# Cross-attention with LoRA on one core: where four of the eight Wkv tiles get their raw weight in the opening

## The reference

```python
def _lora_linear(x, W, A, B):
    return x @ W + 2.0 * (x @ A @ B)
q = _lora_linear(hidden, Wq, Aq, Bq)        # 8 x 256 x 1024
k = _lora_linear(traces, Wk, Ak, Bk)        # 8 x 256 x 256
v = _lora_linear(traces, Wv, Av, Bv)        # 8 x 256 x 256
scores = q @ k.T / sqrt(32)                 # per head
context = softmax(scores) @ v
out = hidden + _lora_linear(context, Wo, Ao, Bo)
```

## Time and profile before

| | |
|---|---|
| median of 3 runs | 675.79 us (675.72 to 678.38) |
| the profiled execution, its own time | 678.06 us |
| its span in the trace | 676.3 us |
| mean granted TensorE clock | 0.947 |
| PE, DVE, ACT, POOL busy | 98%, 76%, 69%, 56% of the span |

### The profile page before, as it was taken

How to read it: one execution, slowest core, us unless ns; L and a number is a source line. 1 busy time by engine, 2 the same in 40 slices (tenths; PEclk the granted TensorE clock), 3 DMA queues, 4 the chain that set the end, 5 groups by cost and what they waited for, 6 DMA issues and landing times.

```text
span 676.3 us, 13385 instructions
## 1 busy us (share of the span) xinstructions
PE 662.5 (98%) x4220; PEld 528.2 (78%) x4220; DVE 512.7 (76%) x1161; ACT 467.6 (69%) x1462; POOL 375.9 (56%) x325
## 2 busy tenths in 40 slices
PE   9999999999999999999999999999899999999998
PEld 6798777877877887887887788787676788888886
DVE  4768887787788778778777877878887898855542
ACT  5558888888888888888888888887678443222220
POOL 3548785843762584386358438535867005776632
PEclk9999999999999999999999999999899999999999
DMA  8956655675665567556656646667676335655331
GB/s 268 355 171 211 207 182 164 196 212 167 174 197 183 158 195 227 162 179 195 198 149 201 210 157 183 197 187 211 186 225 205 107 120 172 202 187 186 126 121 66
DMA packets 103829, 125.07 MB, mean 185 GB/s; under 512 B 9280, under 2 KB 85312, under 8 KB 103760
## 3 DMA queue, kind: packets, MB, share of 16 engines
q1 hardware_dynamic: 103760, 124.23, 59.6%
HBM read 86.18 MB, written 38.01 MB: 184 GB/s over the span
## 4 chain that ended last, share of the span: by engine, by line
PE 82%; DVE 8%; ACT 4%; DMA 3%; issue 2%; SPq 1%; DVEq 0%
PE banks L1484 20%; PE banks L1677 17%; PE banks L1482 10%; PE banks L1502 9%; PE banks L1532 8%; PE banks L1519 8%; PE banks L1543 6%; DVE neg_max L1142 2%; ACT banks L930 2%; PE banks L1463 2%; DVE turned_sb L1163 2%; DMA raw<-xt 1%; PE banks L1450 1%; DVE max_parts L1151 1%; DMA raw<-ct 1%
## 5 line engine op out<-in xcount | busy, mean ns | idle before, releaser
L930 ACT ACTIVATE banks<-banks,neg_max 128x256 f32<-128x256 f32 x512 | 229.9, 452 | 29.8 <-DVE neg_max L1142 24.6
L812 POOL TENSOR_TENSOR q_stack<-turned_sb,head_mask 8x512 fp32r<-8x512 f32 x128 | 136.0, 1062 | 172.8 <-DVE turned_sb L1163 167.1
L1142 DVE TENSOR_REDUCE neg_max<-banks 128x2 f32<-128x512 f32 x256 | 175.0, 686 | 41.9 <-PE banks L1502 38.9
L941 ACT ACTIVATE probs_t<-banks 128x512 f32<-128x512 f32 x256 | 155.0, 605 | 48.4 <-PE banks L1519 48.0
L1484 PE MATMUL banks<-x_both,w_hi 128*128 128x512 f32 x448 | 162.9, 396 | 0.1
L1482 PE MATMUL banks<-x_both,w_lo 128*128 128x256 f32 x448 | 118.6, 280 | 0.0
L1502 PE MATMUL banks<-k_stack,q_stack 96*128 96x256 f32 x512 | 109.8, 296 | 0.7 <-DMA q_stack<-q_parts 0.7
L1502 PEld LDWEIGHTS banks<-k_stack,q_stack 96*128 96x128 f32 x512 | 81.3, 190 | 35.4 <-issue 25.8
L930 ACT ACTIVATION_READ_ACCUMULATOR banks<-banks,neg_max 128x1 f32 x512 | 106.7, 208 | 0.0
L1519 PE MATMUL banks<-q_stack,k_stack 104*128 104x512 f32 x256 | 102.4, 400 | 0.0
L1482 PEld LDWEIGHTS banks<-x_both,w_lo 128*128 128x128 f32 x448 | 84.5, 189 | 9.2
(11 more groups left out here) (156 smaller groups left out, 1154.7 us busy)
## 6 DMA issues: line engine op xcount, KB each, us to landing
q_stack<-q_parts SPq DMA_DIRECT2D x192, 128.0 KB, 3.0
q_parts<-q_stage SPq DMA_DIRECT2D x64, 256.0 KB, 3.5
raw<-ct SPq DMA_DIRECT2D x32, 256.0 KB, 3.5
raw<-xt SPq DMA_DIRECT2D x32, 256.0 KB, 3.8
scales<-r_rows SPq DMA_DIRECT2D x64, 128.0 KB
context<-ctx_stage SPq DMA_DIRECT2D x64, 128.0 KB, 3.7
stage<-xn SPq DMA_DIRECT2D x16, 512.0 KB, 5.4
w_hi<-context SPq DMA_DIRECT2D x14, 512.0 KB, 7.0
```

The lines of the kernel that those rows point to most:

```text
L812: nc.gpsimd.tensor_tensor(q_stack[rows, u % RING, heads], turned_sb[rows, u % 2].unsqueeze(1).broadcast_to([M_ROWS, 2, S]), head_mask[rows ...
L930: last = nc.scalar.activation(score_bank(s)[:, S * h:S * (h + 1)], score_bank(s)[:, S * h:S * (h + 1)], ACT.Exp, bias=neg_max[:, u % 2, i: ...
L941: nc.scalar.activation(probs_t[:, u % 2, t, 2 * hp:2 * hp + 2, :].rearrange("p a b -> p (a b)"), st_bank[j % 2], ACT.Exp, scale=-1.0).then ...
L1142: nc.vector.tensor_reduce(out=neg_max[:, u % 2, 2 * c:2 * c + 2], in_=score_bank(s).rearrange("p (h t) -> p h t", h=2), axis=AXIS, op=ALU. ...
```

## The change

Wkv's tiles 1, 3, 5 and 7 go the second way (PE multiplies only A by B, DVE adds the raw weight, POOL makes the low part); tiles 0, 2, 4 and 6 stay. DVE's order in the opening becomes: `w_total(1)`, `w_low(0)`, `w_total(3)`, `w_low(2)`, `w_total(5)`, `w_low(4)`, context quarters 0 and 1, `w_total(7)`, `w_low(6)`, context quarters 2 and 3. POOL makes the four low parts between its first and its second stack. ACT's order is the same.

```diff
+KV_ADDS = (0, 2, 4, 6)
...
         def pe_adds(f):
-            return f < FOLD_Q or f in (FOLD_Q + 1, FOLD_Q + 3, FOLD_Q + 5, FOLD_Q + 7, FOLD_Q + 8, FOLD_Q + 12)
+            return f in KV_ADDS or f in (FOLD_Q + 1, FOLD_Q + 3, FOLD_Q + 5, FOLD_Q + 7, FOLD_Q + 8, FOLD_Q + 12)
...
             stack_lows(0)
+            for f in range(FOLD_Q):
+                if not pe_adds(f):
+                    w_low(f)
+            pool.wait_ge(w_lo_pool, sums_to(FOLD_Q - 1))
             stack_lows(1)
...
             build_stack(0)
-            for f in range(FOLD_Q):
+            for f in range(0, FOLD_Q, 2):
+                w_total(f + 1)
                 w_low(f)
-                if 2 <= f < 6:
-                    input_low(c_hl, f - 2, c_hi_done, c_ready, f - 1)
+                if f >= 4:
+                    for j in (f - 4, f - 3):
+                        input_low(c_hl, j, c_hi_done, c_ready, j + 1)
             build_stack(1)
```

## The result

The changed kernel takes 678.40 us (median of 18 runs, 678.12 to 680.13), the kernel before 676.12 us in the 18 runs beside it. The ratio is 1.0034, with a 95% interval of 1.0025 to 1.0042, so +2.3 us (+1.7 to +2.8). The forecast was 678.5 us and +2.7 us: it had the sign and the size. The prediction also held that under 0.5% a measurement of this kernel can't tell a change from none; with 18 runs a side the interval for 0.34% leaves out zero. All comparisons are of fast runs; one run of 805 us, of the kernel with the quarters' order alone, counts as slow and is left out.

The account below looks back on a forecast made before the run. Behind the Wkv folds DVE's queue was taken to set PE's pace: 3.6 us of saved PE work becomes waiting, DVE's queue adds 2.7 us, so 675.79 + 2.7 = 678.5 us. The range was 675.8 to 681.4 us.

Parts of the forecast that it names:

- PE's saved work turns into waiting: Wkv folds on PE: 3.6 us of float32 matmuls saved, but k0 waits for context quarter 0 until 15.76 us.
- POOL and DVE exclude each other and take turns: Opening: instructions with two SBUF inputs block each other, up to 1.28 us per collision; quarter 3 ends at 21.3 us.
- The rival in which DVE keeps its turn: Back-to-back context quarters: POOL gets no turn between them, `w_total(8)` at 26.0 to 26.9, +1.5 to +2.3 us; 18%.
- The cast is free: Second stack: DVE's cast L1072 runs beside POOL without waiting, 21.25 to 21.6 us, giving +2.7 us at `w_total(8)`.
- the first rival: Second stack: the cast is excluded too and waits for POOL until 23.8 us; +3.4 us, 679.2 us; 22%.
- The sum: Whole kernel: -3.6 us of PE work all turned into waiting, +2.7 us for DVE's queue, 678.5 us.
- The clock: PE in the opening: rival that its granted clock falls; +4.9 us, 681.4 us; 12%.
- signs of being wrong: `w_total(8)` before 26 us, granted clock of 13 to 30 us below 0.9, or a delay not found again at 50 us.
- The later x loads are free: DMAs: x quarters issued from 15.8 us, not 13.69, cost nothing, covered by DVE's 2.7 us; uncovered, up to 2 us.
- Nothing absorbs the delay: Behind the opening: PE is full from 30 to 50 us, so the +2.7 us stays to the end.

Follow-up runs that it names:

- the quarters' order alone: Kernel before, all eight tiles still added by PE, with DVE's context quarters moved to where the change has them: ratio 1.0004, +0.3 us.
- the change again: The changed kernel measured once more, unaltered, beside three other kernels on one chip: ratio 1.0025 to the kernel before, +1.7 us.
- POOL made to wait: Changed kernel plus waits on POOL: low part 5 until context quarters 0 and 1 are done, low part 7 until 2 and 3: ratio 1.0001, +0.1 us.
- low parts on DVE: Changed kernel with the four new low parts issued on DVE, not on POOL: ratio 1.0013 to the kernel before, +0.9 us.
- cast on ACT: Changed kernel with the second stack's 80x512 cast on ACT, not on DVE: ratio 1.0017 to the kernel before, +1.2 us.
- the change, x later: Changed kernel with k1's high part (ACT), low part (DVE) and `w_total(8)` ahead of the x quarters: ratio 1.0040 to the kernel before, +2.7 us.
- two given tiles alone: The change for tiles 1 and 3 only, DVE's context quarters behind low parts 2, 4, 5 and 6: ratio 0.9988 to the kernel before, -0.8 us.
- the spread x quarters: Tiles 1 and 3 only, k1's low part first, x quarters spread on ACT and DVE: ratio 0.9977 to the kernel before, -1.6 us.

## Why the prediction was right, point by point

- **PE's saved work turns into waiting.** Right. 20 records of L1456 for 28, and k0 starts 3.5 us behind the common event, as forecast (15.76 less 12.31). The folds end at 14.1, 2.2 us behind that event for the forecast 1.2, mostly since in this execution they started 0.8 us later from it; so PE's pause was 1.35 us and not 2.3. Issue of the first x quarter: 15.41, 3.5 us behind it, as forecast too.
- **POOL and DVE exclude each other and take turns.** Right, also where no row had shown it: between two quarters that stood back to back POOL got its turn, twice. Quarter 3 ended 8.7 us behind the event for the forecast 9.0. The rival in which DVE keeps its turn did not occur.
- **The cast is free.** Wrong. This is the step that failed: it took 2.58 us, as the first rival had it. By the rule of the Trainium skill ("SBUF — State Buffer", "Who interferes with whom"), that a copy or cast in a mode using both ports contends with GpSimd and the later of the two waits, the trace agrees, with 0.41 us alone and 2.58, 2.49 and 2.59 us in three traces beside L743 or L744 (the change, the quarters' order alone, the change again). That the cast runs in such a mode no trace says; they show that it waits.
- **The sum came out all the same**, +2.5 us by `w_total(8)` for the forecast 2.7 and the rival's 3.4, since errors met: the size owes something to luck. L744 was sized at 2.5 us behind quarter 3, from a row that itself had waited for DVE's L1074; it ended 2.2 us behind it (20.57 to 22.79). And the quarters ended 0.3 us earlier. From L744's end to the end of the stack's subtraction the rival had 2.2 us, and it took 2.0 (22.79 to 24.78). The cast's rival less these three is 3.4 - 0.3 - 0.3 - 0.2 = 2.6, and 2.5 was measured.
- **The clock.** Forecast at 12% as a rival that costs +4.9 us. It fell in five of the six traces with four tiles and unfilled pauses (mean of 16.9 to 22.6 us: 0.71, 0.50, 0.71, 0.76 and, with POOL made to wait, 0.80; with the low parts on DVE it stayed at 1.00), and in the change it cost nothing that could be measured. The rival's error was its price: it let k1 run whole at half speed and end 3.6 us late. PE was back at full speed near 22.7 us, and ACT had k1's high part done 0.5 us before DVE came to the low part. That margin was small: with less in DVE's way the low part did wait for PE, 0.19 us (cast on ACT) and 0.51 us (the change, x later). One of the prediction's own signs of being wrong, a mean clock below 0.9 between 13 and 30 us, stood at 0.90 in the trace after and at 0.80 in the second one, and was no sign of the time.
- **The later x loads are free.** Right: ACT starts x quarter 0 at 22.59, straight behind k0's high part, with no wait for a DMA.
- **Nothing absorbs the delay.** Right: 2.5 us at `w_total(8)`, 2.4 us at the first `scores_t` (2.9 to the trace without the wait for the DMA), 2.3 us in the time.

What stays open is how the 1.7 us of the new low parts divides between the first pair, the second pair and the stack that comes behind them: their waits follow each other, and no run took away just one of the pairs.

## What to carry to other kernels

Work given to an idle engine is not free if its operands come through something it shares with the engine that sets the pace; look for the rows in which both run, and count each pair of neighbours in the new order, the small casts too. A stall that is removed goes to whoever stands next in the same conflict, so the gain of one fix is bounded by the next partner, and a wait added at the right place can be worth more than one removed. Work saved in front of a landing, a stack or another engine may bring nothing until what comes behind it is reordered: two given tiles alone could not be told from none, and together with the spread x quarters the kernel was 1.6 us faster. And a landmark in a trace, such as one instruction's start, stands for the time only while the order behind it is unchanged.

## What the runs showed of the hardware

PE's granted clock went from 1.00 to 0.50 in the opening of five traces whose longest pause of PE there was 1.35 to 2.06 us, while with the low parts on DVE (pauses of 0.99 and 1.30 us) it stayed at 1.00. It did not fall at the same time in two executions of the same kernel: in one it was at 0.50 from 20 to 22 us, in the other from 17 to 23, with PE busy for most of either. With transposes in the pauses it stayed at 1.00. The trace of the kernel before has 0.95 in every stretch and its repeat 1.00; the span differs by 1.9 us, and nothing in the kernel chose between them. A cast of 80x512 on DVE, from SBUF to SBUF, takes 0.41 us alone and waits for a POOL subtraction of two SBUF tiles to its end, as a subtraction with two SBUF inputs does. DVE's 128x512 instructions with one input in PSUM took 0.67 to 0.69 us beside POOL in the openings of all traces.
